# Two expert steps in every state-space slot, a block's norm beside its predecessor's experts, and the expert weights split two stages earlier

## The reference: what is computed

```python
# layer 1, state space: 512 channels x 16 states, one step in time:
dA = jnp.exp(A[None] * dt[:, :, None])
h = dA * h + dt[:, :, None] * B_t[:, None, :] * x_t[:, :, None]
y = jnp.einsum('bdn,bn->bd', h, C_t) + D * x_t
...
y = y * silu(z);  y = y @ out_proj_w.T + out_proj_b
r = y + residual;  out = layernorm(r) * ln_gamma + ln_beta        # then x = x + out
# layer 1, experts, on xf = layernorm(x)
logits = xf @ gate_w.T + gate_b                                   # rms norm, softmax at 0.5, top 1
norm_g = masked / (masked + 1e-06)
h = gelu(einsum('nd,edh->neh', xf, w1) + b1, approximate=False)   # 8 experts x 512 hidden
y = einsum('neh,ehd->ned', h, w2) + b2
x = x + (y * norm_g[:, None, None]).sum(axis=1)                   # all eight experts are summed
```

## Time and profile before

| | us |
|---|---|
| Median of 3 runs | 2184.84 (2183.36 to 2186.42) |
| The profiled execution's own time | 2185.44 |
| Its span | 2183.7 |
| Busy in it: TensorE / its weight loads | 1416.8 / 797.5 |
| Busy: VectorE / ScalarE / GpSimd | 1399.5 / 970.4 / 716.3 |
| Mean granted TensorE clock | 0.763 of full speed |
| `l0_experts`, first to last instruction | 754.9 to 852.9 |
| `l1_blocks`, first scan / last scan's end / end | 1395.0 / 2031.2 / 2183.7 |

### The profile page before, as it was taken

One profiled execution on the slowest core, in us unless ns is written; L12 is line 12 of the kernel. 1 busy time (PEld: TensorE's weight loads), 2 busy tenths in 40 slices (PEclk: granted clock), 3 DMA queues, 4 the chain that ended last, 5 costly groups with the idle time before them and its releaser, 6 DMA issues. The chain is left out here.

```text
span 2183.7 us, 34795 instructions
## 1 busy us (share of the span) xinstructions
PE 1416.8 (65%) x12500; PEld 797.5 (37%) x12500; DVE 1399.5 (64%) x2490; ACT 970.4 (44%) x1792; POOL 716.3 (33%) x788
## 2 busy tenths in 40 slices
PE   5588733336666596158888178334469759859889
PEld 3334312224444442035555033100135425425556
DVE  1277677772434576747776754599889699698310
ACT  2288622222121211335555243364359649649344
POOL 0043300000002300334343000255469668668533
PEclk7566656667888598579998588555669969959979
DMA  1255300001001000455563133778536446445000
GB/s 68 106 193 192 135 20 0 0 0 44 0 0 39 0 0 16 85 98 96 89 97 68 25 99 84 194 204 205 121 93 152 102 120 147 107 114 128 11 1 10
DMA packets 138252, 177.97 MB, mean 82 GB/s; under 512 B 105503, under 2 KB 110559, under 8 KB 125056
## 3 DMA queue, kind: packets, MB, share of 16 engines
q1 hardware_dynamic: 138116, 176.14, 32.1%
HBM read 138.07 MB, written 14.97 MB: 70 GB/s over the span
## 5 line engine op out<-in xcount | busy, mean ns | idle before, releaser
L2416 POOL TENSOR_TENSOR mf_st<-mf_st,mf_c_rep 128x1024 f32<-128x1024 f32 x128 | 301.4, 2355 | 342.1 <-DVE mf_st L2485 342.1
L2485 DVE TENSOR_TENSOR_SCAN mf_st<-mf_dA,mf_u_ps 128x512 f32<-128x512 f32 x256 | 310.3, 1212 | 16.3 <-ACT mf_dA L2611 16.3
L2325 PE MATMUL mf_y_ps<-mf_st,c_consts 128*32 128x512 f32 x512 | 129.3, 803 | 179.0 <-POOL mf_st L2416 136.8
L2362 PE MATMUL mf_eh<-mf_parts,mf_w 128*128 128x512 f16 x768 | 194.3, 392 | 24.3 <-ACT mf_hT L2640 23.0
L2379 PE MATMUL mf_ey<-mf_w,mf_hid 128*128 128x256 f16 x1536 | 189.1, 274 | 3.6 <-POOL mf_hid L2441 3.6
L2479 DVE TENSOR_TENSOR mf_u_ps<-mf_st,mf_b_ps 128x512 f32<-128x512 f32 x256 | 177.6, 694 | 13.7 <-issue 3.1
L2441 POOL TENSOR_TENSOR mf_hid<-mf_hT,mf_hid 128x512 f16<-128x512 f32 x128 | 147.6, 1160 | 103.4 <-ACT mf_hT L2640 103.3
L2379 PEld LDWEIGHTS mf_ey<-mf_w,mf_hid 128*128 128x128 f16 x1536 | 151.3, 99 | 47.7 <-POOL mf_hid L2441 4.1
L2611 ACT ACTIVATE mf_dA<-c_dt,c_neg_a 128x496 f32<-128x496 f32 x256 | 159.5, 696 | 10.8 <-DVE mf_dA L2569 6.5
L1073 POOL TENSOR_SCALAR mg_we<-mg_we 128x2048 f32<-128x2048 f32 x2 | 10.8, 5382 | 431.9 <-DMA mg_we<-in_l_we 431.9
L1756 ACT ACTIVATE t_p<-t_s_ps,t_mx 128x257 f32<-128x257 f32 x256 | 107.1, 473 | 48.0 <-DVE t_mx L1780 48.0
(11 more groups left out here) (479 smaller groups left out, 2928.9 us busy)
## 6 DMA issues: line engine op xcount, KB each, us to landing
mf_st<-xs SPq DMA_DIRECT2D x64, 1024.0 KB, 7.1
a_ctx_t<-in_ctx_t SPq DMA_DIRECT2D x16, 1024.0 KB, 6.7
a_ctx_n<-in_ctx_n SPq DMA_DIRECT2D x16, 1024.0 KB, 4.9
xs<-mi_xc SPq DMA_DIRECT2D x16, 256.0 KB, 4.1
zs<-mi_sz SPq DMA_DIRECT2D x4, 1024.0 KB, 6.8
mf_r<-in_l_w SPq DMA_DIRECT2D x8, 512.0 KB, 7.9
mf_xq<-xs SPq DMA_DIRECT2D x16, 256.0 KB
mf_zq<-zs SPq DMA_DIRECT2D x16, 256.0 KB
```

The source lines that it names most:

```text
L2325: m = e.matmul(y_ps[T * j:T * j + T, :], c.pick[:, gg, :], st[u % RING][:, j, :], start=(gg == 0), stop=(gg == 3))
L2362: m = e.matmul(bank(b, 5 + at)[:, :], w1[q][w][:, j, f * P:(f + 1) * P], parts[x][:, j, :], start=(j == 0 and w + x == 0), stop=(j == CJ - ...
L2416: e.tensor_tensor(half(u, h), half(u, h), over(c_rep[u // UNITS % 2][:, :], [P, 2, BT], 1), ALU.mult).then_inc(hcs("done"), 1)
L2485: e.tensor_tensor_scan(st[u % RING][:, j, :], dA[:, n % AHEAD, :], u_ps[j % 2][:, :], 0.0, ALU.mult, ALU.add).then_inc(hs("done"), 1)
```

## The change

Four things move.

1. The sixteen weight pieces are split in `l0_experts`: per tile SP loads one piece, ScalarE scales and rounds it (two copies of 128 x 1024), GpSimd subtracts, and SP writes both FP16 halves to DRAM (`ws`). The tile loops are unrolled. `l1_blocks` only loads the halves, two DMAs of 256 KB per slot in slots 0 to 15; `split_weight` and `split_rest` go.
2. The experts run two steps in every slot, from slot FIRST + DELAY = 25 to 88, without a break between blocks. Steps 32b and on of block b begin at its p=7. So p=0 to 6 of block b stand beside the last 14 steps of block b-1. The slots' number goes from 84 to 91.
3. On TensorE a slot is now: hidden, combine, sums, hidden, combine, and only then `project`, `turn` or `logits`. The norm's steps are spread: `residual` at p=1, the first `normalised` at the end of p=1, `gain`, `shift` and `add` on GpSimd at p=2 and 3 between its other work, the second moments at p=3, `normalised` at the end of p=4, `turn` at 5, `logits` and `rest` at 6, the gate at 7, 9, 11, `final(b-1)` at p=8.
4. Buffers: AHEAD 12 to 10, HIDS 5 to 6, `parts` doubled, the gelus' float output in its own `g`, `hT` on top of `r`; the order of the two banks is read from a list (`ring`) made from the slots. The first memset zeroes only the entries of dA that the exp does not write.

```diff
@@ l0_experts
+        @block.sync
+            def fetch(t):
+                if t > 1:
+                    e.wait_ge(w_lo, t - 1)
+                    e.wait_ge(w_hi, 2 * t - 2)
+                source = ...
+                e.dma_start(raw[t % 2][:, :], source).then_inc(w_in[t % 2], 16)
+            fetch(0)
+            for t in range(TILES):
+                if t + 1 < TILES:
+                    fetch(t + 1)
+                e.wait_ge(w_lo, t + 1)
+                for x in range(2):
+                    e.dma_start(c.d["ws"][t, x], split[t % 2][x][:, :]).then_inc(w_out[t % 2], 16)
...
         @block.scalar
+            for t in range(TILES):
...
+                e.wait_ge(w_in[u], (t // 2 + 1) * 16)
+                if t > 1:
+                    e.wait_ge(w_lo, t - 1)
+                    e.wait_ge(w_out[u], t // 2 * 32)
+                e.activation(scaled[u][:, :], raw[u][:, :], ACT.Copy, scale=W_SCALE).then_inc(w_hi, 1)
+                e.activation(split[u][0][:, :], raw[u][:, :], ACT.Copy, scale=W_SCALE).then_inc(w_hi, 1)
+        @block.gpsimd
+                e.wait_ge(w_hi, 2 * t + 2)
+                e.tensor_tensor(split[u][1][:, :], scaled[u][:, :], split[u][0][:, :], ALU.subtract).then_inc(w_lo, 1)
@@ l1_blocks
-RING, AHEAD, HIDS, LAG = 4, 12, 5, 3
+RING, AHEAD, HIDS, LAG = 4, 10, 6, 3
-FIRST = UNITS + 2
+FIRST, DELAY = UNITS + 2, 7
-            at = [0, 2, 5][(p - 4) % 3] + (p - 4) // 3 * 8
-            return range(at, at + (2 if (p - 4) % 3 == 0 else 3)) if p >= 4 else range(0)
+        def hiddens(s):
+            n = 2 * (s - FIRST - DELAY)
+            return (n, n + 1) if 0 <= n < BLOCKS * HIDDEN else ()
+        for s in range(SLOTS):
+            b, p = post(s)
+            ring += [("hidden", n) for n in hiddens(s)]
+            ring += [("out", 2 * b + k) for k in range(2) if p == 0]
+            ring += [("turn", 2 * b + k) for k in range(2) if p == 5]
+            ring += [("logits", b)] if p == 6 else []
...
             def fetch_weight(m):
-                e.wait_ge(*w_hi.at("done", m - 2))
-                e.dma_start(raw(m), source).then_inc(w_in[m % 2], 16)
+                for x in range(2):
+                    e.dma_start(to, c.d["ws"][m, x]).then_inc(w_in[m // 2], 16)
...
         TensorE, per slot
-                if p < 4 and 1 <= s <= N:
-                    sums(s - 1)
-                if live and p == 0:
-                    project(b, 0)
-                    project(b, 1)
...
+                for n in steps[:1]:
+                    hidden(n)
+                    if n >= LAG:
+                        combine(n - LAG)
+                if 1 <= s <= N:
+                    sums(s - 1)
+                for n in steps[1:]:
+                    hidden(n)
+                    if n >= LAG:
+                        combine(n - LAG)
+                if p == 0:
+                    project(b, 0)
+                    project(b, 1)
+                if p == 5:
+                    turn(b, 0)
...
+                if p == 6:
                     logits(b)
-                    bias(b)
...
         GpSimd, per slot
                     weigh(s, 0)
-                if live and p == 1:
-                    affine_add(b)
+                if p == 2:
+                    gain(b)
+                for n in steps[:1]:
+                    low(n)
                     gate((s - 5) // 4)
+                if p == 3:
+                    add(b)
                     weigh(s, 1)
+                if p == 2:
+                    shift(b)
+                if p == 6:
                     rest(b, 0)
                     rest(b, 1)
+                for n in steps[1:]:
+                    low(n)
...
         VectorE, per slot
-                    if j == 1 and 2 <= s < 2 * E + 2:
-                        split_rest(s - 2)
-                    if j == 1 and b > 0 and p == 0:
-                        final(b - 1)
-                    if p == 0 and j == 2:
+                    if p == 1 and j == 0:
                         residual(b)
-                    if p == 1 and j == 1:
+                    if p == 1 and j == 3:
                         normalised(my, my_std, my_normed, b, r)
-                    if p == 2 and j == 2:
+                    if p == 3 and j == 3:
                         e.wait_ge(*affine.at("done", b))
                         moments(e, own, fg_var, fg, c.X[:, rows(b), :])
-                    if p == 3 and j == 1:
+                    if p == 4 and j == 3:
                         normalised(fg, fg_std, fg_normed, b, c.X[:, rows(b), :])
-                    if p == 5 and j == 0:
+                    if p == 7 and j == 0:
                         gate_squares(b)
+                    if p == DELAY + 1 and j == 2 and b > 0:
+                        final(b - 1)
...
+            final(BLOCKS - 1)
...
         ScalarE, per slot: decays(s + 1), then
+                if p == 1:
+                    root(my, my_var, my_std, b)
+                if p == 4:
+                    root(fg, fg_var, fg_std, b)
+                for n in hiddens(s):
+                    gelu(n)
+                if p == 5:
+                    features(b, 0)
+                    features(b, 1)
```

More of the change, by code:

```diff
@@ L2187, in l1_blocks @@
         scale = sb("scale", [E, P])
-        g = [hT[:, u, :] for u in range(2)]
+        g = [sb(f"g{u}", [P, BT]) for u in range(2)]
         hid = [[sb(f"hid{u}{x}", [P, BT], FP16) for x in range(2)] for u in range(HIDS)]
@@ L2218, in post, with freed, bank @@
         def post(s):
[L2220 to L2242 removed]
+            b, p = divmod(s - FIRST, UNITS)
+            return (b, p) if 0 <= b < BLOCKS else (-1, -1)
+        def hiddens(s):
+            n = 2 * (s - FIRST - DELAY)
+            return (n, n + 1) if 0 <= n < BLOCKS * HIDDEN else ()
+        ring = []
+        for s in range(SLOTS):
[4 more added lines that the diff above has]
+            ring += [("logits", b)] if p == 6 else []
+        order = {step: k for k, step in enumerate(ring)}
+        def freed(kind, n):
+            kind, n = ring[order[kind, n] - 2]
+            return {"out": r1, "turn": rounded, "logits": lg_read, "hidden": gelus}[kind].at("done", n)
+        def bank(kind, n):
+            return eh[order[kind, n] % 2]
         def rows(b):
@@ L2285, in fetch_weight, with store @@
             def fetch_weight(m):
-                e.wait_ge(*w_hi.at("done", m - 2))
-                source = c.d["l1_w1"][m // 2].rearrange("p j f -> p (j f)") if m % 2 == 0 else c.d["l1_w2"][m // 2].rearrange("p f o -> p (f o)")
-                e.dma_start(raw(m), source).then_inc(w_in[m % 2], 16)
+                w = w1[m // 2] if m % 2 == 0 else w2[m // 2]
+                for x in range(2):
+                    to = w[x][:, :, :].rearrange("p j f -> p (j f)")
+                    e.dma_start(to, c.d["ws"][m, x]).then_inc(w_in[m // 2], 16)
+            def store(b):
+                e.wait_ge(*added.at("done", b * KT_ + KT_ - 1))
+                e.dma_start(c.d["out"][:, rows(b), :], c.X[:, rows(b), :]).then_inc(stored, 16)
             replicate(0)
@@ L2371, in bias, with combine @@
                              over(c.sm["b2"][0:E, :], [E, 2, C], 1), start=True, stop=False)
-            def combine(b, at):
+            def combine(n):
+                b, at = divmod(n, HIDDEN)
                 q, f = divmod(at, FJ)
-                e.wait_ge(*los.at("done", b * HIDDEN + at))
-                part = hid[(b * HIDDEN + at) % HIDS]
+                if at == 0:
+                    bias(b)
+                e.wait_ge(*los.at("done", n))
+                part = hid[n % HIDS]
                 for k in range(KT_):
@@ L2510, in residual @@
                     x = r[:, 2 * kk:2 * kk + 2, :]
[L2511 removed]
+                    e.tensor_tensor(x, x, bank("out", 2 * b + kk)[:, :].rearrange("p (k f) -> p k f", k=2), ALU.add).then_inc(r1("done"), 1)
                 e.wait_ge(*r1.at("done", 2 * b + 1))
@@ L2645, in root @@
                 e.activation(m.std[:, :], m.var[:, :], ACT.Sqrt, bias=c.eps[:, 0:1]).then_inc(std("done"), 1)
-            for each in (dAs, w_hi, my_std, fg_std, rounded, rms, exps, gelus):
+            for each in (dAs, my_std, fg_std, rounded, rms, exps, gelus):
                 each.start(e)
```

261 lines of the change are left out of this document (99 added, 162 removed).

## The result

| | before | after |
|---|---|---|
| Median, us | 2184.10 (2182.69 to 2186.42) | 2154.36 (2145.26 to 2157.34, 4 runs) |
| Ratio | | 0.9867 [0.9838, 0.9895] |
| Profiled execution's own time | 2185.44 | 2157.34 |
| First scan of unit 0 | 1395.0 | 1391.7 |
| Units 0 to 17 | 157.1 | 145.6 |

A forecast was written before the change was run, and what follows sets the result against it. VectorE was taken as busy in the first 18 units, ScalarE as setting full expert slots. The terms -19.8 - 8.9 - 7.9 - 7.8 + 12.5 + 1 + 4 = -26.9 gave span 2156.8, median 2158 us, range 2142 to 2181.

The forecast's parts named there:

- Weight splitting leaves units 0 to 17: `l1_blocks`, units 0 to 17: without splitting work, 137.3 us against 157.1, -19.8, with nothing taken for transfers.
- DMA short: Rival: transfers do not fit, +7 us in units 0 to 15, up to +11 in `l0_experts`, 2165 to 2176; chance 0.12.
- Block 0: Units 18 to 33, no experts beside the norm: stalls of 4.7 and 3.6, 150.9 us against 159.8, -8.9.
- Block 1: Units 34 to 49: 144.1 us without stalls, new waits of 7.4 and 7.1, 160.6 against 168.5, -7.9.
- Units 50 to 63: These units of `l1_blocks`: bare time, side work and stalls sum to 143.0 us against 150.8, -7.8.
- The tail: After the last scan: eleven more pairs of expert steps, +28.7 us, partly offset by less TensorE idling; +12.5.
- `l0_experts`: Layer 0's experts, which take over the split: TensorE keeps tiles at 5.91 us; +1 for the first landing.
- TensorE's clock: From p=1 to p=4 it may fall to the lower level, making logits late at p=7; +4 us, between 0 and 24.
- signs of being wrong: Units from p=5 over 8.3 us, TensorE's clock below 0.8 over a block, VectorE waiting at p=7, ScalarE waiting in `l0_experts`.
- stalls smaller: Rival: ScalarE and TensorE keep ahead, the two new stalls shrink to half, 2135 to 2148 us; chance 0.15.
- Slower: Rival: TensorE's granted clock falls through all expert slots, +65 us at 0.65, 2222; chance 0.10 with the table case.
- Table switches of 2.66: Rival: ScalarE's table switches make 38 slots take 10.6 us, +100, about 2260; chance 1 in 100.

The follow-up runs named there:

- e3: The changed kernel with a weight piece loaded in every second slot (0 to 30) instead of every slot (0 to 15): 2143.12 us, ratio 0.9820.
- e1: The changed kernel again, unaltered, five times for its spread: 2151.68 us, ratio 0.9868 to the kernel before.
- e9: The kernel before once more, unaltered, one run, to see how much untouched stages vary: 2181.55 us.
- e2: The kernel before with only the weight split moved to `l0_experts`; slots, orders and buffers stay: 2169.59 us, ratio 0.9946.
- e4: The changed kernel with GpSimd's `gain`, `shift` and `add` moved earlier, into p=2: 2144.06 us, ratio 0.9827.
- e7: The changed kernel with e3's spread loads, e4's earlier GpSimd operations, and `residual` last in p=1, first `normalised` at p=2: 2127.07 us, ratio 0.9731.
- e6: e4 with one more wait: GpSimd's second `weigh` of p=3 waits until VectorE's second moments are done: 2138.21 us, ratio 0.9794.
- e11: e7 with one wait more: GpSimd waits for VectorE's second moments ahead of p=3's first `low`: 2111.81 us, ratio 0.9677.
- e10: e7 with second moments in mid p=4, second `normalised` at p=5, and GpSimd waiting for the moments at p=4: 2112.30 us, ratio 0.9673.

## Why the prediction was right, point by point

Predicted was 2158 (2142 to 2181); the median was 2154.36. Direction, size and most of the stages came as forecast; one wait was put at nothing that cost 8 us, and errors of the opposite sign covered it. The steps, in the order of the prediction:

- **Weight splitting leaves units 0 to 17: -19.8 predicted, -11.5 measured.** This is the term that was mis-sized. Its bare sum is right (137.3; e3 took 137.6). What failed is "It fits at 0.86 ... I take nothing": the DMA share was 0.95, states came late, and the stage took 8.3 us more than the bare sum. That is the rival *DMA short*, priced at 7 us by a ceiling on bandwidth. The bandwidth had no such ceiling (223 GB/s against 208); the states, fetched three units ahead, landed late nonetheless. Part of it is a wrong count of bytes: "about 1.66 MB a slot" is too low, since 208 GB/s over 157.1 us in 18 slots are 1.81. Over 137.3 us those are 238 GB/s, and the prediction's own rule of three gives a share of 0.94 and not 0.86. e3 removes the loss by loading the same pieces at half the rate, which shows the cause.
- **Block 0: -8.9 predicted, -9.1 measured.** Units 18 to 33 took 150.7 (150.9; its addends give 150.7). The stalls were not quite those foreseen: 6.4 at p=1 (4.7; 5.8 in e1, 5.2 in e3) and 3.4 at p=3 (3.6).
- **Block 1: -7.9 predicted, -6.4 measured.** 162.1 against 160.6. The two new stalls are 7.15 (7.4) and 6.78 (7.1), where they were foreseen. TensorE began the projection 6.3 us after VectorE's first scan of p=0 (6.7). The first four normalising operations took 4.30 (4.44 was taken); the small ones at p=3 took 1.7 too long (1.0). `final` at p=8 "waits for nothing" by the prediction; it waited 1.74, which is about what block 1 lacks.
- **Units 50 to 63: -7.8 predicted, -7.7 measured.**
- **The tail: +12.5 predicted, +9.9 measured.** TensorE's busy time rose by 22.9, where 28.7 for the extra steps less 4.5 for the clock (24.2) was taken, and its idle time fell from 22.9 to 9.9 (11.2 predicted).
- **`l0_experts`: +1 predicted, 0 measured.** A piece landed in 3.7 and its halves' stores in 2.4, where 5.8 was taken, and tiles stayed at 5.91. ScalarE's three waits for a piece fell in time that it had to spare.
- **TensorE's clock: +4 predicted, 0 seen.** In block 1's norm stretch the window shows the higher of its two levels nearly throughout, 0.93 where the row of before has 0.71; VectorE never waited at p=7 (in the profiles of before it did, for decays).

```profile
1688.00:1743.90 55.90, 44.36 (x231) 22.67 (x229) 41.00 (x60) 35.30 (x48) 39.54 (x23) 0.93 0.37 88
```

- **Nothing foreseen for the stages between: -3.3 measured**, since unit 0 started earlier. It can't be put down to the change: between `l0_experts` and `l1_blocks` the first profile of before took 528.9, e9 (the same kernel) 523.4, and the changed kernel 525.5 and 525.6.

So the loss of 8.3 in the first stage and 1.5 in block 1 was offset by the tail (2.6), the clock (4), `l0_experts` (1) and the unchanged stages (3.3), and 2156.8 met 2155.6. That closeness is luck: errors of about 10 one way met errors of about 11 the other way. e2 shows the same by another cut. The split gained 12.3, where the prediction's terms give 19.8 - 1 = 18.8, and the new schedule 17.9, where they give 8.1. What isn't luck are the places and sizes of the stalls in blocks 1 and 2 and the totals of block 0 and of units 50 to 63.

Of the prediction's signs of being wrong, two came true as they are worded, and neither meant what it was to mean. Units from p=5 on did take over 8.3 us (in block 1 9.3, 10.7, 11.0 and 9.5 at p=7, 8, 9 and 11), because they hold side work of VectorE that the prediction's own sum of 144.1 has in it. And ScalarE did wait for weights in `l0_experts`, at no cost. A sign has to name the quantity that the sum rests on: the bare slots, 7.48, and the tiles, 5.91.

The rival *stalls smaller* did not come true: neither stall shrank to half. *Slower* was wrong in its mechanism: the granted clock in units 34 to 63 is 0.93 and 0.92, not below 0.81. *Table switches of 2.66* fell with the rows: ScalarE spent 115.6 us waiting for VectorE to free an entry of the ring of decays, and no scan waited for a decay, so it didn't set the time of a unit:

```profile
L2638 ACT ACTIVATE mf_dA<-c_dt,c_neg_a 128x496 f32<-128x496 f32 x256 | 167.1, 701 | 116.1 <-DVE mf_st L2527 115.6
```

What the prediction had as a wait at p=3 is only half understood by that word. It was right in size for this kernel. But e4 took the wait away and gained 2.8 per slot instead of 7, because the same backlog of GpSimd then held VectorE inside its small operations. The cost lay in GpSimd's unbroken run of work from p=2 to p=3, and appeared as a wait, as long operations, or (e7) as both. e4 against e6, and e7 against e11, change only whether and where GpSimd pauses in it, and give 1.9 to 3.1 and 2.5 to 5.2 us per slot. From e7 to e11 the p=3 slots of blocks 0 to 2 lose 2.5 + 5.2 + 5.2, p=4 takes 1.3 back twice: 10.3. From the first scan to the last scan's end the two profiles differ by 10.7.

What stays open: in block 1 of e10 the waiting operation got no turn at five ends of GpSimd instructions; in its block 2, with the same instructions at the same distances, and in e4 and e7 each got its turn at the next end. No run tells what decides it. That a hold which starts a little earlier would free p=9 too wasn't tried.

## What to carry to other kernels

When queues are ordered by hand, walk every queue past the moved step with the durations of the old trace: it gave the two new stalls of blocks 1 and 2 to within 0.4 us, and missed by 1.7 block 0's first and the wait of `final`, which was put at nothing. Count the bytes of a stretch from its measured rate and length, and not from the transfers that come to mind. Price a transfer by what else is in flight in the same stretch and not by its bytes: sixteen loads at the rate of the states cost 8 us, the same loads at half the rate none. And when a wait on GpSimd is taken away, look at what its unbroken work does to VectorE's small operations next; here a pause of 0.65 us on GpSimd gave 5.2 us a slot, less 1.3 in the next (e11), the removal of the wait 2.8 (e4).
